# Sums of the rotary embedding moved from GpSimd to VectorE in the beginning of the second attention, with two reorderings around it

## The reference

```
proj = x @ W_in.T + b_in                 # q, k, v: 16 heads of 64
q = _rope(q, sin, cos)                   # y_lo = x_lo*cos + x_hi*sin
k = _rope(k, sin, cos)                   # y_hi = x_hi*cos - x_lo*sin
att = softmax(mask(q @ k.T * scale))
y = att @ v
return y @ W_out.T + b_out
```

## Time and profile before

| | |
|---|---|
| median of 3 executions | 2277.01 us (2276.4 to 2287.38) |
| profiled execution: time / span in the profile | 2284.02 us / 2282.2 us |
| mean granted TensorE clock | 0.941 |
| block in front of the second attention | about 898 to 917 us of the span |
| its prologue, from the first normalized tile to the first stack | about 917 to 968 us |

### The profile page before, as it was taken

How to read it: one execution, slowest core, us unless ns; L and a number is a source line. 1 busy time by engine, 2 the same in 40 slices (tenths; PEclk the granted TensorE clock), 3 DMA queues, 4 the chain that set the end, 5 groups by cost and what they waited for, 6 DMA issues and landing times. The chain is left out here.

```text
span 2282.2 us, 52729 instructions
## 1 busy us (share of the span) xinstructions
PE 1963.1 (86%) x18758; PEld 1402.1 (61%) x18759; DVE 1723.2 (76%) x3728; ACT 1400.1 (61%) x2750; POOL 1025.3 (45%) x1207
## 2 busy tenths in 40 slices
PE   6988999889825996487899999999999999459999
PEld 4666666666623664165677777777767677336665
DVE  8878888888772443487688887878797968679997
ACT  4666666666642443286678786969687879244343
POOL 5434454343032001689757475757675753132222
PEclk9999999999757998799999999999999999769999
DMA  7000000000153332012100000000000000100000
GB/s 245 2 2 2 2 1 2 2 1 2 32 180 90 87 93 62 1 18 36 15 2 2 2 2 1 2 1 2 1 2 2 2 2 2 39 1 16 16 18 24
DMA packets 53369, 57.77 MB, mean 25 GB/s; under 512 B 7104, under 2 KB 47376, under 8 KB 53152
## 3 DMA queue, kind: packets, MB, share of 16 engines
q1 hardware_dynamic: 46528, 45.79, 6.3%
q0 software_dynamic: 6416, 8.95, 1.9%
q10 hardware_dynamic: 208, 0.11, 0.0%
HBM read 36.22 MB, written 18.61 MB: 24 GB/s over the span
## 5 line engine op out<-in xcount | busy, mean ns | idle before, releaser
L371 PE MATMUL a_bank<-w_in_sb,xnT_sb 128*128 128x512 f16 x1152 | 288.6, 389 | 33.8 <-DVE t_buf_sb L579 28.1
L531 DVE TENSOR_REDUCE neg_max_sb<-a_bank 128x1 f32<-128x128 f32 (+3 forms) x512 | 236.0, 482 | 91.4 <-PE a_bank L288 90.0
L1209 DVE TENSOR_REDUCE neg_max_sb<-a_bank 128x1 f32<-128x128 f32 (+3 forms) x512 | 235.9, 484 | 81.7 <-PE a_bank L938 77.6
L1098 ACT ACTIVATE probT_sb<-a_bank 128x512 f32<-128x512 f32 (+1 forms) x384 | 198.7, 526 | 144.4 <-PE a_bank L961 139.5
L442 ACT ACTIVATE p_hi_sb<-a_bank 128x384 f16<-128x384 f32 (+1 forms) x384 | 204.9, 534 | 120.9 <-PE a_bank L297 119.2
L434 ACT ACTIVATE prob_sb<-a_bank,neg_max_sb 128x128 f32<-128x128 f32 (+3 forms) x512 | 260.8, 542 | 22.7 <-DVE neg_max_sb L531 21.8
L538 DVE TENSOR_TENSOR p_lo_sb<-a_bank,p_hi_sb 128x384 f16<-128x384 f32 (+1 forms) x384 | 227.9, 595 | 60.7 <-ACT p_hi_sb L442 57.0
L453 ACT ACTIVATE stack_sb<-a_bank 128x1024 f16<-128x1024 f16 (+1 forms) x256 | 211.1, 825 | 7.1 <-PE a_bank L342 6.7
L297 PE MATMUL a_bank<-ident_f_sb,prob_sb 128*128 128x128 f32 x1280 | 206.9, 277 | 3.7 <-DVE p_lo_sb L538 3.1
L707 POOL TENSOR_TENSOR rope_w_sb<-t_buf_sb,sin_sb 128x256 f32<-128x256 f32 x128 | 146.4, 1144 | 134.6 <-DVE t_buf_sb L579 132.4
L371 PEld LDWEIGHTS a_bank<-w_in_sb,xnT_sb 128*128 128x128 f16 x1152 | 104.1, 99 | 140.6 <-DVE t_buf_sb L579 35.9
(11 more groups left out here) (272 smaller groups left out, 5608.5 us busy)
## 6 DMA issues: line engine op xcount, KB each, us to landing
sorted_rows<-zeros_sb SPq DMA_DIRECT2D x1, 4992.0 KB, 22.7
x_in_sb<-sorted_rows SPq DMA_DIRECT2D x39, 128.0 KB, 2.2
sorted_results<-y_moe_sb SPq DMA_DIRECT2D x39, 128.0 KB, 1.7
x_sb_sb<-L_attn_x SPq DMA_DIRECT2D x8, 512.0 KB, 9.7
w_raw_sb<-L_ffn_gate_bank SPq DMA_DIRECT2D x8, 512.0 KB, 3.8
w_raw_sb<-L_ffn_up_bank SPq DMA_DIRECT2D x8, 512.0 KB, 4.8
w_raw_sb<-L_ffn_down_bank SPq DMA_DIRECT2D x8, 512.0 KB, 5.8
out<-x_sb_sb SPq DMA_DIRECT2D x32, 128.0 KB, 1.7
```

The costliest lines, as they stand in the source:

```text
L371: last = pe.matmul(out, xnT[:, x, c, j * P:(j + 1) * P], w["in"][:, w_, c, cols], start=k == 0, stop=k == len(terms) - 1)
L531: last = dve.tensor_reduce(neg_max[:, i:i + 1], S[(3 * h + g) % 2][:, off:off + L], AX.X, ALU.max, negate=True)
L1098: act.activation(probT[:, (h // 4) % 2, h % 4, T_AT[r]:T_AT[r + 1]], ST[(3 * h + r) % 2][:, 0:T_AT[r + 1] - T_AT[r]], ACT.Exp).then_inc(s_ ...
L1209: last = dve.tensor_reduce(neg_max[:, h % 2, i:i + 1], S[(3 * h + g) % 2][:, off:off + L], AX.X, ALU.max, negate=True)
```

## The change

- In the prologue of layer 1's attention the eight sums `rope_z` are made by VectorE (`rope_sum`), one piece behind its takes; GpSimd makes only the two products of a piece and the low part of the piece before. A new semaphore `s_w` counts the products. Outside the prologue nothing changes.
- In the block in front VectorE makes the low weights first and the statistics after them.
- In the first attention `w_out_raw` is counted with identities and mask on one semaphore, so TensorE now also waits for `w_out_raw` before its first stack.

```diff
@@ vector, prologue
             for p in range(PIECES):
                 take("piece", 0, 0, p)
+                if L1 and 1 <= p <= 8:
+                    rope_sum(p - 1)
...
+        def rope_sum(p):
+
+            wait(dve, s_w, p + 1)
+            wait(dve, s_u, p + 1)
+            wait(dve, s_piece, p - 1)
+            dve.tensor_tensor(rope_z[:, p % 2, :, :], rope_u[:, p % 2, :, :], rope_w[:, :, :], ALU.add).then_inc(s_z, 1)
@@ gpsimd, rotate(b, half, p, prologue=False)
-            own(pool.tensor_tensor(rope_w[:, :, 32:64], src[:, :, 0:32],
-                                   sin[:, 32:64].unsqueeze(1).to_broadcast([P, 8, 32]), ALU.mult))
+            second = pool.tensor_tensor(rope_w[:, :, 32:64], src[:, :, 0:32],
+                                        sin[:, 32:64].unsqueeze(1).to_broadcast([P, 8, 32]), ALU.mult)
+            if prologue:
+                second.then_inc(s_w, 1)
+                return
+            own(second)
@@ gpsimd, prologue
-                    rotate(0, 0, p)
-                    piece_lo(0, 0, p)
+                    rotate(0, 0, p, True)
+                    if p:
+                        piece_lo(0, 0, p - 1)
+                    if p == PIECES - 1:
+                        piece_lo(0, 0, p)
@@ first attention
-            pe.wait_ge(s_small, 48)
+            pe.wait_ge(s_small, 64)
...
-            act.wait_ge(s_w, 16)
+            act.wait_ge(s_small, 64)
@@ l1_attention, vector
-            partial_stats(dve, 0)
-            variances(dve, GROUP_A)
             for c in range(C):
                 dve.wait_ge(s_hi, c + 1)
                 dve.scalar_tensor_tensor(out=w_in[:, 1, c, :], in0=w_raw[:, c, :], scalar=W1_SCALE,
                                          in1=w_in[:, 0, c, :], op0=ALU.mult, op1=ALU.subtract)
+            partial_stats(dve, 0)
+            variances(dve, GROUP_A)
             invert(dve, GROUP_A)
```

More of the change, by code:

```diff
@@ L204, in attention @@
     s_z = sem("rope_ready")
+    s_w = sem("rope_sin_ready")
     def work(k, last):
@@ L694, in take, with rotate @@
             fin.then_inc(s_piece, 1)
-        def rotate(b, half, p):
+        def rotate(b, half, p, prologue=False):
             t, j = piece_parts(p)
@@ L836, in attention0 @@
     s_ident = sem("ident_f_loaded")
-    s_w = sem("out_weights_loaded")
-    s_small = sem("masks_loaded")
+    s_small = sem("out_weights_and_masks_loaded")
     s_alibi = sem("alibi_loaded")
@@ L1437, in prologue @@
                 pool.dma_start(dst[:, :], src).then_inc(s_small, 16)
-            pool.dma_start(w_out_raw[:, :, :], d["w_out0"].rearrange("(c p) n -> p c n", p=P)).then_inc(s_w, 16)
+            pool.dma_start(w_out_raw[:, :, :], d["w_out0"].rearrange("(c p) n -> p c n", p=P)).then_inc(s_small, 16)
             pool.memset(one[:, :], 1.0).then_inc(s_const, 1)
```

## The result

| | before | changed |
|---|---|---|
| median of 11 executions | 2286.31 us | 2272.0 us |
| lowest and highest | 2276.4, 2293.51 | 2264.69, 2276.66 |
| profiled execution, its span | 2284.02, 2282.2 | 2276.33, 2274.5 |
| granted clock of TensorE, mean | 0.941 | 0.939 |

The ratio is 0.9943, 95% interval 0.9923 to 0.9963: 13.0 us less, between 8.5 and 17.6. The two medians lie 14.3 us apart; the savings in this text that come from timings are worked out from the ratio. The profiled execution of before is not among its eleven. The three executions known when the forecast was made are among the eleven of before.

What follows compares the result with a forecast made beforehand. GpSimd was taken to bound the second attention's prologue, VectorE's order the block in front. Savings of 9.8 and 3.2 us, together 13.0, were subtracted from the median 2277.01, giving 2264.0 us; range 2257 to 2270.

Steps and rivals of the forecast that it cites:

- the base: Whole kernel: the time the saving was subtracted from, the median of 2277.01 us, not the profiled 2284.02.
- The prologue: Second attention's prologue: GpSimd loses eight sums and the waits for ScalarE; 9.8 us saved, bounds 5.2 to 16.6.
- The walk through the new ring: Prologue: one piece followed through GpSimd's products, low part and VectorE's sum; 3.58 us per round, ScalarE's high part hidden.
- the hand-over from the sum to the next product: Prologue, each round: from the end of VectorE's sum to GpSimd's next product, 0.07 us.
- The low weights: Block in front: low weights before the statistics bring the reciprocal's end forward; 3.2 us saved, bounds 1.35 to 6.1.
- Three rules: Block's indirect DMAs beside low weights: nothing held, 6.1 us saved; 0.53 each, 4.5; held to the instruction's end, 3.2 (taken).
- the list of signs: Trace signs of being right: VectorE's sums 1.2 to 1.8 us, rounds 3.5 to 3.7, two indirect DMAs 3 instead of 1.5.
- The joined semaphore: First attention's first stack: also waiting for `w_out_raw` costs nothing, with 15 us of cover.
- Not held: Rival, block in front: indirect DMAs aren't held, 6.1 us saved there instead of 3.2, total 2261.1 us; chance 0.12.
- the sums hide: Rival, prologue: VectorE's instructions fit GpSimd's gaps, rounds near 2.6 us, 19.8 saved in all, 2257.2 us; chance 0.13.
- dearer ports: Rival: rounds of 4.27 us, DMAs held once or thrice; 6.6 to 8.4 saved, counted as no change; chance 0.22.
- Slower by TensorE's clock: Rival, 976 to 1100 us: granted clock falls from 0.94 to 0.76, kernel 11 us slower, near 2288 us; chance 0.03.

Runs made afterwards that it cites:

- experiments 1 to 4: Kernel before with, in turn: low weights ahead of statistics, 0.9997; new prologue only, 0.9945; later low part only, 0.9983; prologue sums on VectorE only, 0.9993.
- experiments 5 to 8: Changed kernel with, in turn: low weights cut, 0.9961; cosine product from PSUM, 0.9934; cut weights and low part on VectorE, 0.9911; nothing altered, 2264.0 us.
- experiment 8: The changed kernel run once more, unchanged, one execution with its trace: 2264.0 us.
- experiment 1: Kernel before with only the low weights moved ahead of the statistics in the block in front: median 2285.76 us, ratio 0.9997.

## Why the prediction was right in its parts and wrong in its time

**The step that failed is the base.** The prediction said "so I subtract from the median" of 2277.01, because "both cuts are far from what differs between executions". That median came from three executions, two of which were among the quickest that before ever showed: eleven give 2286.31, 9.3 us more, 29 more on the chip of experiments 1 to 4 give 2286.43 between 2274.99 and 2293.57, and 11 on that of experiments 5 to 8 give 2283.29. The forecast's own 13.0 taken from 2286.31 is 2273.3; measured were 2272.0. The range of 2257 to 2270 was made from the terms of the saving alone and had no term for the base, though the executions at hand, the profiled one among them, lay 11 us apart, nearly as wide as the range of 13. In relative terms 0.57% was forecast and 0.57% measured by the ratio (0.63% by the two medians); with an interval of 9 us, an agreement to the tenth is luck, and what bears the forecast out are the places in the traces, 12.7 us.

The base goes with TensorE's granted clock over the execution: of those 29, the eight at 0.932 to 0.934 average 2291.8 and the five at 0.940 to 0.943 average 2280.9. The changed kernel's eleven show the same: 2276.06 to 2276.66 at 0.939, 2264.69 at 0.948. Where it comes from is seen in the traces alone: the stretches at 1.2 GHz in the two attentions, which differ between executions of one kernel (experiment 8).

**The prologue**, forecast 9.8, measured 9.32. The prediction read a wait of 1.26 for ScalarE into every round; q pieces, with one high part instead of two, had 0.74. The walk through the new ring doesn't rest on it and held step by step: sums of 1.62 (1.2 to 1.8 expected), second product 1.18, cosine product squeezed in, high part hidden until the last piece. The term that was too small is the hand-over from the sum to the next product, put at 0.07: from the sum's end (930.32 + 1.62 = 931.94) to 932.08 are 0.14. That makes the round 3.66 instead of 3.58.

**The low weights**, forecast 3.2, measured 3.35. The statistics start 13.02 us after ScalarE's first high part, where the walk had 13.11 (911.15 - 898.04). Three rules stood against each other, nothing held, 0.53 each, to the end of the instruction; 3.04 and 2.96 beside instructions of 3.3 leave only the third. (Held were the third and the fourth of the four DMAs, as in the walk; the list of signs says second and last.) The Trainium skill, "SBUF — State Buffer", section "SBUF: two separate sides", calls the shared ports a lock held for the whole instruction: the traces agree. The same page, section "Who interferes with whom", infers that an instruction of VectorE with two inputs in SBUF leaves GpSimd's descriptors alone. The prediction took the 0.53 of the earlier trace rows for a disagreement; neither that nor the 3.04 is shown to be one. What is held lies in the first 0.13 us of a DMA: the one of 901.45 was issued 0.13 us ahead of the first low part (901.58) and took its usual 1.56, 1.43 of it beside that instruction, and the held one of 903.31 ended 1.50 after the second low part had begun (904.86). The positions are read from SBUF, so the hold may be that read; that it is this read no run isolates.

**The joined semaphore**, forecast 0. The wait in front of the first attention's first stack has the same releaser as before. It was not undone by itself.

**The rivals.** *Not held* falls with experiment 1, *the sums hide* with rounds of 3.66, *dearer ports* with the same. *Slower by TensorE's clock* did not come: in 976 to 1100 it was granted 0.93 after 0.94. But a weaker form of it, which I had not priced, is in the timings: short stretches at 1.2 GHz deep in the dense part, 0 to 17.1 us of the second attention, different in two executions of one kernel.

## What to carry to other kernels

Take the base of a forecast with the same care as its terms: if a handful of executions lie as far apart as the saving is large, give the saving as a difference and let the range hold the spread; and before a loss elsewhere in the trace of the changed kernel is put down to the change, look at the same stretch in a second trace of the same kernel. Where GpSimd and VectorE work side by side on SBUF, count the pair as one queue for VectorE's instructions with two inputs there and GpSimd's, cut the long ones into pieces when another engine's short step waits behind them, and let one input come from PSUM where the value lies there anyway. A ring over three engines gets shorter by staggering it (5.7 us here) and by moving a step to the engine on which it is cheap (3.8, and 5.0 more with the low part moved too).

## What the runs showed of the hardware that I had not expected

- An indirect DMA of GpSimd is held until the running two-input instruction of VectorE ends, 1.5 us more beside one of 3.3, though the next such instruction is queued behind it; the hold touches only its first 0.13 us, and a DMA that is past them runs beside the instruction at 1.56.
- TensorE fell to 1.2 GHz for 0 to 17.1 us in the attention, not in the same way in two executions of one kernel (0 and 17.1), at 0.3 us lost for each, and always right behind the one wait of 1.90 us that a batch element has: 22 of the 60 such waits in ten traces were followed by a fall.
- In the new prologue TensorE works less per piece than it waits, yet its granted clock was 1.00 from 931 to 956 (0.95 over the 931 to 968 of the earlier trace rows, instead of 0.77), and groups of six matmuls took 1.47 us each:

```profile
936.26 1.47 PE L372 MATMUL a_bank<-w_in_sb,xnT_sb 128*128 128x512 f16 x6 [2.19 <-DVE t_buf_sb L580]
```

In the trace of before the same groups took from 1.47 to 2.74. Nothing shows that it shortened the ring, whose rounds GpSimd and VectorE set.
